# Graph layer on one core: the tensor product built with features on partitions, from spherical rows loaded repeated

## The reference, cut to what matters

```python
def tensor_product(x_e, sh, w, C):            # C is [64, 9, O]
    acc = sh[:, 0:1] * (x_e @ C[:, 0, :])
    for s in range(1, S):
        acc = acc + sh[:, s:s + 1] * (x_e @ C[:, s, :])
    return acc * w
k = tensor_product(x_dst, edge_sh, wk, Cqk).reshape(-1, H, DQK)
v = tensor_product(x_dst, edge_sh, wv, Cv).reshape(-1, H, DV)
attn = jnp.einsum('ehd,ehd->eh', q[edge_src], k)
```

## Time and profile before

| what | value |
|---|---|
| median of 3 runs | 3732.7 us (3731.88 to 3733.3) |
| the profiled execution | 3729.88 us, its span 3728.2 us |
| PE busy over the span | 3330.0 us (89%) |
| PEld, DVE, ACT, POOL busy | 85%, 77%, 34%, 55% |
| DMA moved | 622.16 MB, mean 167 GB/s |

### The profile page before, as it was taken

How to read it: one execution, slowest core, us unless ns; L and a number is a source line. 1 busy time by engine, 2 the same in 40 slices (tenths; PEclk the granted TensorE clock), 3 DMA queues, 4 the chain that set the end, 5 groups by cost and what they waited for, 6 DMA issues and landing times. The chain is left out here.

```text
span 3728.2 us, 86642 instructions
## 1 busy us (share of the span) xinstructions
PE 3330.0 (89%) x25947; PEld 3178.9 (85%) x25947; DVE 2877.5 (77%) x5292; ACT 1285.0 (34%) x3333; POOL 2055.4 (55%) x1999
## 2 busy tenths in 40 slices
PE   2099999999999337999999999999999999999963
PEld 1088888888888237999999999999999999999953
DVE  4366666666666227999999999999999999999943
ACT  1033333333333113444444444444444444444420
POOL 2577777777777435555555555555555555555540
PEclk9599999999999658999999999999999999999975
DMA  8399999999999313444444444444444444444420
GB/s 339 86 268 280 279 279 279 279 280 279 279 280 279 105 46 105 127 126 132 131 124 129 131 129 124 130 132 126 125 132 132 124 128 131 130 124 129 132 78 29
DMA packets 843789, 622.16 MB, mean 167 GB/s; under 512 B 490431, under 2 KB 732803, under 8 KB 843452
## 3 DMA queue, kind: packets, MB, share of 16 engines
q1 hardware_dynamic: 667110, 500.09, 44.2%
q0 software_dynamic: 56640, 87.65, 9.7%
q10 hardware_dynamic: 119982, 33.79, 4.1%
HBM read 335.87 MB, written 286.31 MB: 167 GB/s over the span
## 5 line engine op out<-in xcount | busy, mean ns | idle before, releaser
L1305 POOL DMA_INDIRECT xg<-h_tab,src_i x808 | 861.5, 1066 | 220.8 <-issue 127.2
L789 POOL DMA_INDIRECT kv<-kv_tab,src_i x808 | 762.1, 943 | 285.7 <-issue 188.2
L1315 POOL TENSOR_TENSOR kq<-kvs,q_of 128x512 f32<-128x512 f32 x202 | 260.6, 1290 | 837.7 <-DVE kvs L1491 837.7
L1401 ACT ACTIVATE z_hi<-bank 128x512 fp32r<-128x512 f32 x808 | 439.4, 595 | 802.9 <-PE bank L1333 802.9
L1357 PE MATMUL bank<-C_hi,z_hi 128*128 128x256 f32 x4040 | 682.2, 299 | 0.0
L1357 PE MATMUL bank<-C_lo,z_hi 128*128 128x256 f32 x4040 | 612.2, 281 | 0.0
L1481 DVE TENSOR_TENSOR z_lo<-bank,z_hi 128x512 fp32r<-128x512 f32 x808 | 520.5, 686 | 113.5 <-ACT z_hi L1401 113.4
L1357 PEld LDWEIGHTS bank<-C_hi,z_hi 128*128 128x128 f32 x4040 | 537.8, 191 | 0.3
L1357 PEld LDWEIGHTS bank<-C_lo,z_hi 128*128 128x128 f32 x4040 | 535.3, 188 | 0.0
L1357 PE MATMUL bank<-C_hi,z_lo 128*128 128x256 f32 x3232 | 516.2, 281 | 0.0
L913 DVE TENSOR_TENSOR wsb<-bank,b 128x512 f32<-128x512 f32 x404 | 279.3, 691 | 298.7 <-PE bank L977 298.3
(11 more groups left out here) (248 smaller groups left out, 4754.4 us busy)
## 6 DMA issues: line engine op xcount, KB each, us to landing
w_tab<-wsb SPq DMA_DIRECT2D x202, 512.0 KB, 3.4
win<-w_tab SPq DMA_DIRECT2D x202, 512.0 KB, 3.6
sum_edge<-rowt SPq DMA_DIRECT2D x202, 288.0 KB, 2.5
q_edge<-zq SPq DMA_DIRECT2D x202, 256.0 KB
qs<-q_edge SPq DMA_DIRECT2D x202, 256.0 KB, 2.8
sum_edge<-rows ACTq DMA_DIRECT2D x202, 136.0 KB
qs<-q_edge SPq DMA_DIRECT2D x202, 128.0 KB
drow<-dst_tab SPq DMA_DIRECT2D x202, 128.0 KB, 3.2
```

The costliest lines, as they stand in the source:

```text
L789: pool.indirect_dma_start(kv[b][:, q, :], None, kv0_tab, bass.IndirectOffsetOnAxis(ap=src_i[:, i * Q + q:i * Q + q + 1], axis=0))\
L1305: pool.indirect_dma_start(xg[b][:, q, :], None, h1_tab, bass.IndirectOffsetOnAxis(ap=src_i[:, i * Q + q:i * Q + q + 1], axis=0))\
L1315: pool.tensor_tensor(kq[:, :].rearrange("p (q o) -> p q o", q=Q), kvs[b][:, :, 0:O1], q_of[b % 2][:, :].rearrange("p (q o) -> p q o", q=Q) ...
L1401: nc.scalar.activation(z_hi[b % 2][:, k, :], bank[ZB[k]][:, :], ACT.Copy).then_inc(hi_out, 1)
```

## The change

The tensor product of the fourth stretch is made with features on partitions from the start:

- PE turns the gathered x rows (`turn_x`, two transposes a step), and ACT copies them into `xT` twice, for both halves of the partitions (`take_x`, four copies of 64x256). 18 transposes of z go.
- The spherical values arrive turned and repeated: `sh_tab` holds, per step, 8 rows of 512 values, and `load_sh` reads rows of it into 64 partitions at once, two loads of 64 x 8 KB and two of 64 x 1 KB a step in place of one load of 18 KB. `outer` and `outer_last` multiply on DVE with all partitions in features.
- `hi` and `lo` take z from SBUF, in two pieces of 128x1024 and a ninth part, in place of four of 128x512 and a ninth part.
- `same` is built on ACT (`apart`: four Squares of 128x128, `build`: one Relu of 128x512), no longer on DVE.
- `spread_q` has a bank of its own. The order of the stages on PE, ACT and DVE is new; `outer_last` comes before `outer(0)`, and `logits` after `lo(1)` and `product(0)`.
- The two tables are made in the third stretch: SP loads the spherical rows with 101 steps on partitions, ACT rearranges them (`sh_parts`) between its copies of `crows` and of `wvT`, and SP stores them. Each half is `SG` = 101 steps, and one `sh_parts` buffer serves both.

```diff
+            SG = NST // 2
+            sh_rows = [sb(f"sh_rows{g}", [SG, ST, S], F32, ph) for g in range(2)]
+            sh_parts = sb("sh_parts", [SG, S, ST], F32, ph)
@@ third stretch, SP
+                    def load_sh_rows(a):
+                        last_full = (NST - 1) * ST
+                        sp.dma_start(sh_rows[0][:, :, :], a[0:SG * ST, :].rearrange("(p e) s -> p e s", p=SG))\
+                          .then_inc(sh_rows_in, 16)
+                        sp.dma_start(sh_rows[1][0:NST - 1 - SG, :, :],
+                                     a[SG * ST:last_full, :].rearrange("(p e) s -> p e s", e=ST)).then_inc(sh_rows_in, 16)
+                        sp.dma_start(sh_rows[1][NST - 1 - SG:NST - SG, 0:TAIL, :], a[last_full:E, :].unsqueeze(0))\
+                          .then_inc(sh_rows_in, 16)
+
                     load_last_rows(sp, lrows, sum0_edge, last_got)
+                    sp.wait_ge(sh_padded, 1)
+                    sp.sem_inc(sh_rows_turn, 1)
+                    with sp.If(flag > 0):
+                        load_sh_rows(ea9_s)
+                    with sp.Else():
+                        load_sh_rows(ea9)
                     sp.wait_ge(zeros_set, 1)
...
                     sp.dma_start(car[:, :, :], carry0_tab[0:N, :].rearrange("(p j) d -> p j d", j=NJ)).then_inc(car_got, 16)
+                    for g in range(2):
+                        sp.wait_ge(sh_parts_set, g + 1)
+                        sp.dma_start(sh_tab[g * SG:(g + 1) * SG], sh_parts[:, 0:S - 1, :]).then_inc(sh_put, 16)
+                        sp.dma_start(sh_last_tab[g * SG:(g + 1) * SG, :], sh_parts[:, S - 1, :]).then_inc(sh_put, 16)
                     sp.wait_ge(h1_ready, 1)
@@ third stretch, ACT, behind the copies of crows and ahead of those of wvT
+                    act.wait_ge(sh_rows_in, 48)
+                    for g in range(2):
+                        if g:
+                            act.wait_ge(sh_put, 32)
+                        for r in range(2):
+                            nc.scalar.activation(sh_parts[:, 4 * r:4 * r + 4, :],
+                                                 sh_rows[g][:, :, r:S - 1:2].rearrange("p e c -> p c e"), ACT.Copy)
+                        for r in range(2):
+                            ins = nc.scalar.activation(
+                                sh_parts[:, S - 1, r * ST // 2:(r + 1) * ST // 2].rearrange("p (h e) -> p h e", e=P),
+                                of_half(sh_rows[g][:, :, S - 1], r), ACT.Copy)
+                        ins.then_inc(sh_parts_set, 1)
@@ fourth stretch, SP
+                        need(sp, z_last_ready, i - 1)
+                        for f, e in zip(rows_of, edges_of):
+                            sp.dma_start(sh_last[b % 2][f, :], sh_last_tab[bass.ds(i, 1), e].broadcast_to([D, ST // 2]))\
+                              .then_inc(sh_in[b % 2], 16)
+
+                        need(sp, z_ready, i * 2 - 2)
+                        for r, f in enumerate(rows_of):
+                            sp.dma_start(sh[b % 2][f, :, :].rearrange("p c e -> p (c e)"),
+                                         sh_tab[bass.ds(i, 1), 4 * r:4 * r + 4, :].rearrange("a c e -> a (c e)")
+                                         .broadcast_to([D, 4 * ST])).then_inc(sh_in[b % 2], 16)
@@ fourth stretch, PE
-                    pipelined(pe, [(t_z(0), 1), (t_z(1), 1), (turn_max, -2), (sums, -3), (m_acc(0), 0), (t_z(2), 1),
-                                   (t_z(3), 1), (m_acc(1), 0), (t_z(4), 1), (spread_q, 0), (m_acc(2), 0),
-                                   (turn_logits, -1), (m_acc(3), 0)], RING)
+                    pipelined(pe, [(turn_x, 3), (turn_max, -2), (sums, -3), (m_acc(0), 0), (m_acc(1), 0), (spread_q, 0),
+                                   (m_acc(2), 0), (turn_logits, -1), (m_acc(3), 0)], RING)
@@ fourth stretch, ACT
+                    def take_x(it, i, b):
+                        act.wait_ge(x_mm, i + 1)
+
+                        need(act, z_ready, i * 2 - 2)
+                        for f in rows_of:
+                            for r, g in enumerate(rows_of):
+                                ins = nc.scalar.activation(of_half(xT[b % 2][f, :], r),
+                                                           bank[b % 2][g, 0:2 * P].rearrange("p (h e) -> p h e", e=P), ACT.Copy)
+                        ins.then_inc(x_out, 1)
-                    pipelined(act, [(hi(0), 1), (hi(1), 1), (copy_max, -2), (weights, -2), (take_sums, -3), (hi(2), 1),
-                                    (hi(3), 1), (hi(4), 1), (take_q, 0)], RING)
+                    pipelined(act, [(hi(0), 1), (copy_max, -2), (weights, -2), (take_x, 3), (take_sums, -3), (hi(1), 1),
+                                    (apart, 1), (hi_last, 1), (take_q, 0), (build, 1)], RING)
@@ fourth stretch, DVE
+                        def stage(it, i, b):
+                            dve.wait_ge(x_out, i + 1)
+                            dve.wait_ge(sh_in[b % 2], 64 * (2 * it + b // 2 + 1))
+
+                            need(dve, lo_out, i * 3 - 5 + k)
+                            c = slice(2 * k, 2 * k + 2)
+                            dve.tensor_tensor(z[b % 2][:, c, :], bcast(xT[b % 2][:, :], 1, 2), sh[b % 2][:, c, :], ALU.mult)\
+                               .then_inc(z_ready, 1)
-                    pipelined(dve, [(product(1), -1), (lo(0), 1), (lo(1), 1), (subtract, -2), (outer(0), 2), (lo(2), 1),
-                                    (lo(3), 1), (logits, -1), (weigh, -2), (outer(1), 2), (lo(4), 1), (build, 1),
-                                    (segment_max, -1), (product(0), 0)], RING)
+                    pipelined(dve, [(product(1), -1), (subtract, -2), (outer_last, 2), (outer(0), 2), (weigh, -2), (lo(0), 1),
+                                    (lo(1), 1), (product(0), 0), (logits, -1), (outer(1), 2), (lo_last, 1),
+                                    (segment_max, -1)], RING)
```

169 lines of the change are left out of this document (86 added, 83 removed).

## The result

The changed kernel takes **3814.4 us** (median of 4 runs, 3800.1 to 3825.39) against 3732.29 us before: a ratio of 1.0219, 95% interval 1.0196 to 1.0242. It is slower by about 2%. The forecast was 3661 us with chances of 0.73 for faster. The profiled execution took 3800.1 us, its span is 3798.4 us, 70.2 us longer than that of the kernel before.

What follows compares the result with a forecast made beforehand. PE was taken to bound the kernel, DVE close behind. 3728.2 - 202 (edge steps) + 3 (fill) + 127 (node stretch) = 3656.2 us of span, 3661 us as the median; range 3500 to 3800.

Steps and rivals of the forecast that it cites:

- What bounds the kernel: Second layer's edge stretch: PE sets the pace, busy 500.00 of 500 us, DVE close behind at 467.84; a step is 10.68 us.
- PE's part: Edge step: dropping transposes saves 1.8 us, `turn_x` gives 0.22 back; PE's work falls from 10.68 to 9.1 us.
- DVE's part: Edge step: DVE's instructions in the new order sum to 9.19 us, slightly longer than PE's 9.1.
- rival C: Edge step: POOL becomes the bound, `times_q` held out by DVE's two-input work up to 2.9 us; 3806 us, chance 0.14.
- ACT's part: Edge step: DVE waits 0.49 us at lo(1) for ACT's hi(1), making the step 9.68 us; gain 202 us.
- Other waits: Edge step: remaining waits have slack; DMA needs 7.7 of 9.68 us, 2.9 for the repeated rows; fill 3 us longer.
- The node stretch: Third stretch, tables: 101 rows use one DMA engine at 25.6 GB/s, delaying `wvT` to 1425; costs 127 us, 110 to 145.
- B: Node stretch: the 101-row transfers spread over all engines, so nothing is paid; time 3534 us, chance 0.14.
- D: Edge stretch: one row read 64 times slows loads, DMA sets the pace; 4230 us, deciding from 117 GB/s down, chance 0.15.
- wrong altogether: Edge stretch sign against the whole prediction: a step above 10.05 us, or a clock below full because PE now pauses.

Runs made afterwards that it cites:

- thin loads: The changed kernel with its two large loads a step cut from 8 KB to 512 B into each of 64 partitions: 3746.2 us, ratio 1.0037.
- both causes out: The changed kernel with node-stretch rows split at 96, large loads cut to 512 bytes a partition and POOL's `kq` times 1.0, not q: 3558.83 us.
- one input: The changed kernel with POOL's product `kq` multiplying by 1.0 in place of q, so reading one SBUF tensor: 3834.98 us.
- rows split alone: The changed kernel with the tables' loads and stores of 101 and 100 rows each split into 96 and the rest: 3688.51 us, ratio 0.9893.

## Why the prediction was wrong, by its own steps

**What bounds the kernel, and PE's part.** Right. PE's instructions fell, PE was no longer the bound (449.31 of 500 us busy, 9.25 a step for the 9.1 of the sum), and its clock stayed at 1.00.

**DVE's part.** The step that failed is "outer(0) 1.13 (1.22 less 0.09)". It was priced by a row in which nothing with two inputs ran on POOL. It took 1.88 us on average and 2.08 in the step shown, since the new order puts it behind `subtract` and `outer_last`, where POOL's `kq` starts. The working sees the meeting: rival C names it, with outer(0) as the place. But it lets DVE hold POOL out, for 2.9 us; in the trace POOL keeps its 1.28 us and DVE pays 0.87 of the 1.00 us that the two share. The other way round is there too: the gather at 2503.37, 0.12 us behind `outer(1)`, takes 1.91 us, and `outer(1)` keeps its 1.21. In both rows the one that starts second pays. The Trainium skill, page "VectorE: DVE Perf Modes", section "Two Vector instructions with no wait between them", was cited there for a shared second read interface; with `kq` beside z the trace agrees, and it doesn't say who waits. With 0.87 more in this term, DVE's sum is 10.06, and the gain of the edge stretch is 0.61 x 202 = 123 us, not 202. The run with thin loads measures 10.04. The other terms of the sum held together, as the 9.70 us of the run with both causes out shows, some a little short and the wait for ACT too long.

**ACT's part.** Right, and hidden. The wait for `hi(1)` vanished behind the longer outer(0) and came back, 0.22 for 0.49 us, when that was repaired. `z_hi` at 1060 ns is the 1.06 of the sum. ACT's rest did end ahead of the step.

**Other waits.** The step that failed is "five engines moved 128 GB/s ..., 25.6 each, so sixteen would take 2.9 us". The store of `h1_tab` has 125 rows in 125 partitions; the rows of `sh` go into 64. The rate of an engine was carried over from one set of partitions to another. Measured were 5.0 us in place of 2.6 for the two big loads, so DMA needed 10.4 in place of 7.7, and there it is a bound of its own. The share of 0.54 in the thin run, 5.4 us, bears out the other term, 4.8 for what was there before and an estimated 0.5 (0.2 MB at 410 GB/s) for the small loads that stayed.

**The sum of both.** The two bounds are near each other, 10.04 for DVE and an estimated 9.8 to 10.4 for DMA, and the kernel pays 10.29: DVE's longer product and, in some steps, a wait for DMA on top. That is why taking the one away alone gained nothing (one input: 3795 at the least), and the other alone 68 us (thin loads: 3746).

**The node stretch.** Right in mechanism and nearly in size. One engine for 101 rows: share 0.06 at 27 GB/s where 25.6 was worked out. `wvT` was forecast at 1425 and came at 1433.66, the stretch was to cost 127 us and cost 136.5. The term that was too small is ACT's pass: 1.9 us for each strided copy of 101x2048, where 3.78 were measured (7.55 for two), so 4.6 became 8.5. Only the second pass costs that: the first, which ends near 1343, hides behind the transfers, since `car` lands at 1355.90 (forecast 1348) and the 1.86 MB of the store follow only then, at 27 GB/s. The store was through by 1425.12, forecast 1421. The last 2.7 us lie behind `wvT`, where 2 were forecast. The bounds of 110 to 145 held.

**The rivals.** B didn't come. C came with the other engine as victim, and POOL never was the bound (330.29 of 500 us). D's place was right, outer waiting for a DMA at a full share, and its mechanism wrong: rows of their own are as slow as one row repeated. D had its deciding point at 117 GB/s for the loads of `sh`; they ran at 197, and yet the kernel fell to the slow side. That is an error in D's own sum: it takes 1.18 MB for the whole of DMA's step and leaves out the 4.8 us of other transfers that the working adds under "Other waits". With them a step of 10.05 leaves 5.25 us for the 1.18 MB, and the deciding point is 225 GB/s, above the 197 measured. So D's case was far less remote than its 117 made it look. The range of 3500 to 3800 missed the 3814.4 by 14 us. It left D out, and it took the two troubles of the edge stretch, C and D, as alternatives. They came together. That the miss is no more than 14 us says nothing for the working: the step was 10.29 us, past the 10.05 that it named as wrong altogether.

**Slower at all?** Node stretch +136.5, fill +4.4, steps -75, the new distance between a step's products +3.7: of its forecast gain of 202 us the change lost 0.61 us a step, 123 us, to two causes, and paid the node stretch on top. With the rows split alone it was 1.1% faster than before (0.6 to 1.5).

## What to carry to other kernels

A DMA is priced by its shape on both sides, not by its bytes: how many engines its slowest dimensions allow (101 and 2 were the traps here), and which partitions it lands in (0 to 63 with 64 to 127 as two loads cost twice what 32 to 95 or all 128 do). When an order is changed, list for each product with two SBUF inputs what runs on POOL beside it. And where two bounds lie within a few per cent, a run that takes one away can show little or nothing (here nothing, and 68 us); take both away, then give each back.
